# Expert blocks of 64 rows, two experts to a step in the column halves of TensorE

## The reference, cut to what matters

```python
x = x + _L1_ffn_ref(_layernorm(x), ...)      # x is 8 x 100 rows of 512

def _L1_ffn_ref(x, gate_w, gate_b, bias, w1, b1, w2, b2):
    E, TOP_K, D, H = (8, 2, 512, 352)
    xf = x.reshape(-1, d)                                      # 800 rows
    scores = xf @ gate_w.T + gate_b + bias
    top_scores, top_idx = jax.lax.top_k(scores, TOP_K)         # two experts for each row
    gates = jax.nn.softmax(top_scores, axis=-1)
    comb = jnp.sum(jax.nn.one_hot(top_idx, E) * gates[..., None], axis=1)
    h = jax.nn.silu(jnp.einsum('td,ehd->teh', xf, w1) + b1)
    y = jnp.einsum('teh,edh->ted', h, w2) + b2
    return jnp.einsum('ted,te->td', y, comb)
```

## Time and profile before

| what | value |
|---|---|
| median of 3 runs | 660.88 us (657.59 to 663.14) |
| the profiled execution's own time | 661.93 us |
| its span, first to last instruction | 660.0 us |
| PE busy | 553.8 us, 84% of the span |
| DVE busy | 360.5 us, 55% |
| ACT busy | 267.8 us, 41% |
| POOL busy | 194.6 us, 29% |
| mean granted TensorE clock | 0.913 of full speed |

### The profile page before, as it was taken

One profiled execution on the slowest core, in us unless ns is written; L12 is line 12 of the kernel. 1 busy time (PEld: TensorE's weight loads), 2 busy tenths in 40 slices (PEclk: granted clock), 3 DMA queues, 4 the chain that ended last, 5 costly groups with the idle time before them and its releaser, 6 DMA issues.

```text
span 660.0 us, 10081 instructions
## 1 busy us (share of the span) xinstructions
PE 553.8 (84%) x3342; PEld 341.3 (52%) x3342; DVE 360.5 (55%) x989; ACT 267.8 (41%) x611; POOL 194.6 (29%) x237
## 2 busy tenths in 40 slices
PE   4889695999999999869998998998840699999980
PEld 2454343545555555436766776676630455555540
DVE  4453777667676685267778677777353222222210
ACT  1027771412222232158988677775310122222220
POOL 1010303123123321143446455542705021221220
PEclk9969986999999999979999899896755799999996
DMA  8994770322231200130533123312513245445425
GB/s 324 298 419 119 253 235 0 128 94 70 93 129 51 93 1 0 61 111 13 189 99 111 54 58 111 100 57 83 159 45 103 66 82 96 77 86 97 75 39 131
DMA packets 32663, 72.74 MB, mean 110 GB/s; under 512 B 4042, under 2 KB 19434, under 8 KB 30562
## 3 DMA queue, kind: packets, MB, share of 16 engines
q1 hardware_dynamic: 28198, 63.48, 29.6%
q0 software_dynamic: 4416, 8.63, 8.1%
HBM read 46.40 MB, written 27.33 MB: 112 GB/s over the span
## 4 chain that ended last, share of the span: by engine, by line
PE 59%; DVE 19%; DMA 7%; issue 5%; POOL 4%; ACT 4%; SPq 1%; POOLq 0%; DVEq 0%; ACTq 0%
PE ps L818 9%; PE ps L1123 8%; PE ps L1109 8%; PE ps L812 7%; PE ps L893 4%; DMA w1s<-in_win 4%; PE ps L952 4%; PE ps L876 4%; PE ps L1055 3%; DVE sN L1449 2%; PE ps L944 2%; PE ps L965 2%; ACT hTe L781 1%; POOL g L497 1%; DVE VS L1190 1%
## 5 line engine op out<-in xcount | busy, mean ns | idle before, releaser
L812 PE MATMUL ps<-CT,wkS 128*128 128x364 f32 x224 | 77.8, 501 | 9.3 <-DMA wkS<-in_wk 9.3
L728 ACT ACTIVATE pE<-sN,nmx 100x361 f32<-100x361 f32 x128 | 77.7, 607 | 6.2 <-DVE nmx L1449 6.1
L818 PE MATMUL ps<-wvS,CT 128*121 128x512 f32 x168 | 77.0, 607 | 0.0
L1449 DVE CUSTOM_DVE_ANT_0 sN<-ps,maskS 100x361 f32<-100x361 f32 x128 | 62.0, 531 | 11.3 <-PE ps L944 5.8
L952 PE MATMUL ps<-ident,pE 100*121 100x100 f32 x384 | 63.2, 294 | 1.3 <-ACT pT L719 1.1
L606 POOL DMA_INDIRECT sums_out<-yb,backI x20 | 31.1, 1554 | 109.7 <-ACT yb L791 105.7
L952 PEld LDWEIGHTS ps<-ident,pE 100*121 100x121 f32 x384 | 51.9, 200 | 21.5 <-issue 20.2
L812 PEld LDWEIGHTS ps<-CT,wkS 128*128 128x128 f32 x224 | 44.7, 204 | 35.6 <-issue 14.8
L1123 PE MATMUL ps<-VS,hTe 118*128 x120 | 56.7, 609 | 5.5 <-ACT hTe L781 5.5
L719 ACT COPY pT<-ps 121x300 f32<-121x300 f32 x128 | 51.8, 404 | 22.5 <-PE ps L952 22.3
L1574 DVE TENSOR_TENSOR hb<-ps,b1B 128x352 f32<-128x352 f32 x20 | 10.5, 524 | 88.2 <-PE ps L1109 88.2
(11 more groups left out here) (248 smaller groups left out, 958.5 us busy)
## 6 DMA issues: line engine op xcount, KB each, us to landing
slots_in<-zeros SPq DMA_DIRECT2D x8, 1848.0 KB, 8.9
VS<-in_w SPq DMA_DIRECT2D x6, 1024.0 KB, 30.1
CT<-in_ew SPq DMA_DIRECT2D x8, 704.0 KB
VS<-in_ew SPq DMA_DIRECT2D x8, 672.0 KB
xin<-slots_in SPq DMA_DIRECT2D x20, 264.0 KB, 2.8
CT<-in_ctxT SPq DMA_DIRECT2D x7, 728.0 KB, 11.9
ahead<-in_w SPq DMA_DIRECT2D x2, 1024.0 KB, 34.0
summB<-summary_rows SPq DMA_DIRECT2D x8, 200.0 KB
```

The source lines that it names most:

```text
L728: act.activation(pE[0:S, q, 0:T], sN[0:S, q, 0:T], ACT.Exp, scale=-1.0, bias=nmx[0:S, h_:h_ + 1], accum_out=sums[0:S, j, h_:h_ + 1]).then_ ...
L812: mm = pe.matmul(ps[:, at, 0:TP], wkS[:, k, m * P:(m + 1) * P], ctx(b)[:, k * TP:(k + 1) * TP], start=(k == 0), stop=(k == KC - 1))
L818: mm = pe.matmul(ps[0:TC, at, :], ctx(b)[:, k * TP + c * TC:k * TP + (c + 1) * TC], wvS[:, k, :], start=(k == 0), stop=(k == KC - 1))
L1449: dve.tensor_tensor_reduce(out=sN[0:S, q, 0:T], in0=ps[0:S, q, 0:T], in1=maskS[0:S, j, 0:T], scale=-1.0, scalar=3.4e38, op0=ALU.add, op1=A ...
```

## The change

A block is now 64 rows (`BR`), and there are `(1600 + 8 * 63) // 64 = 32` of them. A step handles two blocks, in general of different experts: the first in rows 0 to 63, the second in rows 64 to 127 of the same tiles. So there are `STEPS = 16` steps in place of 20. Each half has its own matrix products, with 64 stationary columns and its own weights; the first half's weights are addressed through a register as before, the second half's are first copied by VectorE to `w1B` and `w2B`. Since a step can now hold the same row twice (once for its first expert and once for its second), the second choice is added to rows of their own (`SECOND` onward in `sums_out`, zeroed early), and both parts are read to SBUF, added and stored at the end, in two column pieces (70% and 30%). The regions of `slots_in` are laid out anew: 13 blocks of 64 rows for each expert in place of 7 of 128.

```diff
+BR = P // 2
+NBLK = (B * S * TOPK + E * (BR - 1)) // BR
+STEPS = NBLK // 2
-RB = B * S // P + 1
+RB = -(-B * S // BR)
+SECOND = B * S + P
+LIN = B * S * D // P
+LIN_CUT = LIN * 7 // 10
...
+            sp.dma_start(sums_out[SECOND:SECOND + B * S].rearrange("(p r) (q c) -> p (r q) c", r=10, q=2),
+                         zeros[0:B * S // 10, 0:D // 2].unsqueeze(1).to_broadcast([B * S // 10, 20, D // 2]))\
+              .then_inc(sem("slots_zero"), 16)
...
-            for s in range(NBLK):
+            for s in range(STEPS):
                 if s > 1:
                     sp.wait_ge(sem("x_taken"), s - 1)
-                load_block(s)
+                load_block(s, 0)
+                load_block(s, 1)
...
-            sp.dma_start(out.rearrange("b s d -> (b s) d"), sums_out[0:B * S]).then_inc(sem("x_kept"), 16)
-            sp.wait_ge(sem("x_kept"), 16 * (B + 1))
+            for i, at in enumerate(lin_parts):
+                sp.dma_start(x_lin[:, at], linear(sums_out[0:B * S])[:, at]).then_inc(sem(f"x_in{i}"), 16)
+                sp.dma_start(s_lin[:, at], linear(sums_out[SECOND:SECOND + B * S])[:, at]).then_inc(sem(f"x_in{i}"), 16)
+            for i, at in enumerate(lin_parts):
+                sp.wait_ge(sem("x_taken"), STEPS + i + 1)
+                sp.dma_start(linear(out.rearrange("b s d -> (b s) d"))[:, at], x_lin[:, at]).then_inc(sem("x_kept"), 16)
+            sp.wait_ge(sem("x_kept"), 16 * (B + 2))
...
                     for k in range(KC):
-                        mm = pe.matmul(ps[:, 2 + j, 0:EH], xT[:, j, k, :], CT[:, e, k * EH:(k + 1) * EH],
-                                       start=(k == 0), stop=(k == KC - 1))
+                        for w, rows in zip((CT[:, e, k * EH:(k + 1) * EH], w1B[:, j, k * EH:(k + 1) * EH]), halves):
+                            mm = pe.matmul(ps[rows, 2 + j, 0:EH], xT[:, j, k, rows], w,
+                                           start=(k == 0), stop=(k == KC - 1))
...
                     for c in range(3):
-                        mm = pe.matmul(ps[:, 7 - j, :], hTe[0:EC, 1 - j, c, :], vs(e)[0:EC, c * D:(c + 1) * D],
-                                       start=(c == 0), stop=(c == 2))
+                        for w, rows in zip((vs(e)[0:EC, c * D:(c + 1) * D], w2B[0:EC, 1 - j, c * D:(c + 1) * D]), halves):
+                            mm = pe.matmul(ps[rows, 7 - j, :], hTe[0:EC, 1 - j, c, rows], w,
+                                           start=(c == 0), stop=(c == 2))
...
+                ch(dve.scalar_tensor_tensor(out=z[0:S, lo:hi, C_TOK:ZW], in0=hot[0:S, 1, lo:hi], scalar=float(SECOND),
+                                            in1=z[0:S, lo:hi, C_TOK:ZW], op0=ALU.mult, op1=ALU.add))
...
             def copy_x(s, j):
                 dve.wait_ge(sem("x_turned"), s + 1)
-                dve.tensor_copy(xT[:, j].rearrange("p k s -> p (k s)"), ps[:, j, :]).then_inc(sem("xT"), 1)
+                dve.tensor_copy(xT[:, j].rearrange("p k s -> p (k s)"), ps[:, j, :])
+                e = block_expert(mybir.EngineType.DVE, s, 1)
+                if s > 1:
+                    dve.wait_ge(sem("h_mm"), s - 1)
+                dve.tensor_copy(w1B[:, j], CT[:, e, 0:KC * EH]).then_inc(sem("xT"), 1)
...
                 if within(s, 0):
-                    e = block_expert(mybir.EngineType.DVE, s)
-                    take_x(s, j, e)
+                    es = [block_expert(mybir.EngineType.DVE, s, half) for half in range(2)]
+                    for half, rows in enumerate(halves):
+                        take_x(s, j, es[half], rows, half)
+                    if s > 1:
+                        dve.wait_ge(sem("y_mm"), s - 1)
+                    dve.tensor_copy(w2B[0:EC, j], vs(es[1])[0:EC, 0:3 * D])
                     alone(dve, ("h_mm", s + 1))
-                    dve.tensor_tensor(hb[:, j], ps[:, 2 + j, 0:EH], b1B[:, e, :], ALU.add).then_inc(sem("h_biased"), 1)
+                    for half, rows in enumerate(halves):
+                        ins = dve.tensor_tensor(hb[rows, j], ps[rows, 2 + j, 0:EH], b1B[rows, es[half], :], ALU.add)
+                    ins.then_inc(sem("h_biased"), 1)
...
+            for i, at in enumerate(lin_parts):
+                dve.wait_ge(sem(f"x_in{i}"), 32 * (STEPS // 2) + 32)
+                dve.tensor_tensor(x_lin[:, at], x_lin[:, at], s_lin[:, at], ALU.add).then_inc(sem("x_taken"), 1)
```

More of the change, by code:

```diff
@@ L161, in block_kernel @@
         need, own = sb(rr, "need", [P, 6, E]), sb(rr, "own", [1, E])
-        blk_e, blk_p, blk_q, blk_no = (sb(rr, n_, [1, NBLK, E]) for n_ in ("blk_e", "blk_p", "blk_q", "blk_no"))
         blk_f = sb(rr, "blk_f", [1, 4, NBLK])
@@ L197, in block_kernel @@
         xin, xT = sb(cc, "xin", [P, 2, ZW]), sb(cc, "xT", [P, 2, KC, P])
-        vacant = sb(cc, "vacant", [P, NBLK])
-        share, backI = sb(cc, "share", [P, NBLK]), sb(cc, "backI", [P, NBLK], I32)
+        vacant = sb(cc, "vacant", [P, STEPS])
+        share, backI = sb(cc, "share", [P, STEPS]), sb(cc, "backI", [P, STEPS], I32)
         hb, hs, hTe = sb(cc, "hb", [P, 2, EH]), sb(cc, "hs", [P, 2, EHP]), sb(cc, "hTe", [P, 2, 3, P])
         yb = sb(cc, "yb", [P, 2, D])
+        w1B, w2B = sb(cc, "w1B", [P, 2, KC * EH]), sb(cc, "w2B", [P, 2, 3 * D])
+        blk_e, blk_p, blk_q, blk_no = (sb(cc, n_, [1, NBLK, E]) for n_ in ("blk_e", "blk_p", "blk_q", "blk_no"))
         cc.close()
@@ L250, in blocks @@
         def blocks(body):
-            for s in range(NBLK + 1):
+            for s in range(STEPS + 1):
                 body(s, s % 2, s // 2)
@@ L258, in within, with block_expert @@
         def within(s, ahead):
-            return s + ahead < NBLK
-        def block_expert(engine, s):
-            return nc.values_load(blk_x[0:1, bass.ds(s, 1)], engines=[engine], min_val=0, max_val=E - 1,
+            return s + ahead < STEPS
+        halves = (slice(0, BR), slice(BR, P))
+        x_lin = XR[:].rearrange("p b d -> p (b d)")
+        s_lin = z[:].rearrange("p b w -> p (b w)")
+        lin_parts = (slice(0, LIN_CUT), slice(LIN_CUT, LIN))
+        def block_expert(engine, s, half):
+            return nc.values_load(blk_x[0:1, bass.ds(2 * s + half, 1)], engines=[engine], min_val=0, max_val=E - 1,
                                   skip_runtime_bounds_check_because="it is a count held to E - 1 when made")
@@ L393, in _, with load_block, linear @@
             keep_x(B - 1)
[L395 to L396 removed]
+            def load_block(s, half):
+                n = nc.values_load(blk_r[0:1, bass.ds(2 * s + half, 1)], engines=[mybir.EngineType.SP], min_val=0, max_val=E * RB,
                                    skip_runtime_bounds_check_because="it is a sum held to E * RB when made")
[L398 removed]
+                sp.dma_start(xin[halves[half], s % 2], slots_in.rearrange("(n p) w -> n p w", p=BR)[n]).then_inc(sem(f"x_in{s % 2}"), 16)
             sp.wait_ge(sem("block_table"), 1)
             sp.wait_ge(sem("sent"), 16 * TOPK * B)
[L402 removed]
+            for s in range(STEPS):
                 if s > 1:
                     sp.wait_ge(sem("x_taken"), s - 1)
[L405 removed]
+                load_block(s, 0)
+                load_block(s, 1)
+            def linear(rows):
+                return rows.rearrange("r d -> (r d)").rearrange("(p c) -> p c", p=P)
             for j in range(2):
[L408 to L410 removed]
+                sp.wait_ge(sem(f"y_out{j}"), 16 * (STEPS // 2))
+            for i, at in enumerate(lin_parts):
[5 more added lines that the diff above has]
+            sp.wait_ge(sem("x_kept"), 16 * (B + 2))
         @block.gpsimd
@@ L600, in _ @@
             g.wait_ge(sem("x_kept"), 16 * B)
-            for t in range(NBLK):
+            for t in range(STEPS):
                 g.wait_ge(sem("y_copied"), t + 1)
@@ L1532, in _ @@
             dve.wait_ge(sem("counts"), 1)
-            ch(dve.tensor_scalar(need[:, 0], ps[:, 4, 0:E], 1.0 / P, 0.5 - 0.5 / P, ALU.mult, ALU.add))
+            ch(dve.tensor_scalar(need[:, 0], ps[:, 4, 0:E], 1.0 / BR, 0.5 - 0.5 / BR, ALU.mult, ALU.add))
             ch(dve.tensor_scalar(need[:, 1], need[:, 0], MAGIC, None, ALU.add))
@@ L1559, in copy_x @@
                 dve.wait_ge(sem("x_turned"), s + 1)
-                dve.tensor_copy(xT[:, j].rearrange("p k s -> p (k s)"), ps[:, j, :]).then_inc(sem("xT"), 1)
-            def take_x(s, j, e):
-                dve.tensor_copy(share[:, s:s + 1], xin[:, j, bass.ds(D + e, 1)])
-                ch(dve.tensor_scalar(vacant[:, s:s + 1], xin[:, j, C_TOK:C_TOK + 1], 0.0, part[:], ALU.is_equal, ALU.mult))
-                dve.tensor_scalar(backI[:, s:s + 1], xin[:, j, C_TOK:C_TOK + 1], vacant[:, s:s + 1], -1.0, ALU.add, ALU.add)\
-                   .then_inc(sem("x_taken"), 1)
+                dve.tensor_copy(xT[:, j].rearrange("p k s -> p (k s)"), ps[:, j, :])
@@ new lines, in copy_x, with take_x @@
+                e = block_expert(mybir.EngineType.DVE, s, 1)
+                if s > 1:
+                    dve.wait_ge(sem("h_mm"), s - 1)
```

(9 more changed lines are left out.)

41 lines of the change are left out of this document (19 added, 22 removed).

## The result

The changed kernel took 652.16 us (median of 4 runs, 648.73 to 654.12) against 661.01 for the kernel before (4 runs, 657.59 to 663.14). The ratio is 0.9861 [0.9826, 0.9897], so 1.0 to 1.7% faster. The profiled execution took 654.12 us, with a span of 652.3, which is 7.7 less than the 660.0 of before. It was the slowest of its four, so 7.7 is less than the 8.9 between the medians.

What follows compares the result with a forecast made beforehand. The loop was taken as bound by TensorE, 6.19 us a step. -111.4 + 14 x 6.4 + 2.6 + 0.3 + 10.0 = -8.9 us took the profiled 661.93 to 653.0, median 652.0; range 645 to 668.

Steps and rivals of the forecast that it cites:

- The sum: Whole kernel: loop, start and end terms together give -8.9 us, for a median of 652.0 us.
- 1 and 2, fewer steps and P: Loop: 18 periods of 6.19 us become 14 of P, the step time, 6.4 us with paired halves priced as one.
- 3, VectorE: Loop: added copies, bias and `take_x`, 3.1 us more against 4.5 of waiting, cost nothing; slack before the product 0.5 us.
- the slow price of `w2B`: VectorE in a step: this copy at the two-tensor operation's rate, about 1.8 us in place of 0.98.
- 4, the scatter: GpSimd: waiting for the previous scatter's landing costs nothing, since two are 5.54 us apart at the end, below the step time.
- 5, ahead of the loop: Before the loop: added operation, second load, weight copies, second bias and clock cost 2.6 us in all, between 1.5 and 4.
- 6, behind the loop: After the loop: bias and width change 0.3 us; reading, adding and storing both parts 17.2 for 7.5, taken as 10 more.
- the lag of passes: Loop products: second half's first record waits for the first half's second; step 7.1 us, +9.8, 662 us; chance 0.12.
- the partial overlap: L1109 and L1123: halves overlap only in part; at x = 0.26 the step is 7.7 us, total 670; chance 0.12.
- VectorE was not late: Loop: rival that slow or blocked copies make `xT` last; step 6.7 to 7.0 us, 656 to 660 us; chance 0.10.
- The end was cheaper and not dearer: After the loop: rival that the end costs 14 to 16 us in place of 10, 656 to 658; chance 0.08.
- slower by 1%: Loop: outcome given to halves overlapping only in part, 1% lost at a step of 7.5 us; chance 0.12.

Runs made afterwards that it cites:

- free scatters: Changed kernel without a scatter's wait for the landing of the one before, with separate spare rows for empty places of odd steps; 651.81 us, ratio 0.9838.
- the kernel with two copies: Changed kernel with another copy of w1B's size, to a tile nobody reads, made ahead of w1B in each step; 657.07 us in one run.
- the kernel with early copies: Changed kernel with w1B and w2B copied ahead of the bias's wait, and for the first two blocks ahead of the loop; 649.89 us, ratio 0.9839.
- the kernel with the second array alone: Kernel before, still 20 steps of 128 rows, with only second choices added to their own array and the changed kernel's end; 671.54 us, ratio 1.0161.
- the one with four pieces: Changed kernel with the final add cut into four column pieces (40, 30, 20 and 10%) in place of two; 650.52 us in one run.
- a half in a row: Changed kernel with all products of a step's first half issued before those of the second, in place of alternating; 673.29 us in one run.
- the warm clock: Changed kernel with idle TensorE products, eleven before the first turning of x and two behind the second block's; 650.14 us, ratio 0.9827.
- two by two: Changed kernel with products ordered two of the first half, then two of the second, in place of one and one; 655.09 us in one run.
- the combined kernels: Changed kernel with early weight copies after the sends, 12 and 2 idle products, and non-waiting scatters; 644.65 us with two end pieces, 643.22 with four.

## Why the prediction was right

**The sum** gave -8.9 and the span shows -7.7; 652.0 was forecast and 652.16 measured. The loop, the largest term, was right by its mechanism and its size. Two terms around it were off, by +2.4 ahead of it and -1.2 behind, and half cancelled. That the median came within 0.2 us is luck: the executions of either kernel lie 5.4 us apart and more.

**1 and 2, fewer steps and P.** The term of the loop was right within 0.1 us, but not by its parts. The pair at the price of one was right, and the rows on mixing were good evidence for it, though with quarters. P was 6.29 and not 6.4. The change of width that is exposed cost 0.16 us, which the gap of 0.14 us behind the mixing had foretold well; the covered one cost nothing, as reckoned, and the second product became 0.05 shorter, which I hadn't reckoned. The 1.5 us saved so were used up by the second block's product at half the clock: from it to the second product of block 0 are 5.36 us, in a steady step 3.49 (554.71 to 558.20 in the chain), so 1.9 lost, of which 0.2 are lost at the full clock too (3.72 us with free scatters). I had put the clock into the start's term and not after it.

**3, VectorE.** `w1B` took 894 ns for a predicted 920 and `w2B` 961 for 980, the bias 0.52 each. The slack, 0.5 in the prediction, is 0.63 to 0.7 by the kernel with two copies. The copies cost nothing in the loop, which the kernel with early copies shows as well. Two figures of that part were added up carelessly: the work that VectorE gets more is 3.0 us by its own terms and not 3.1, and the slow price of `w2B` would be 1.7 and not 1.8. Nothing hangs on either.

**4, the scatter.** No cost in the loop, as predicted. At the end the wait for the landing before does cost 1.7 us. The kernel before waits for a landing there too, so it isn't part of the change.

**5, ahead of the loop.** Mis-sized: +5.0 for +2.6, beyond the 4 that I had as the upper bound. Of it 1.5 are there at the cast of `slotI` (498.15 for 496.63). The added operation can make 0.22 of these. The other 1.3 are no cost of the change that any run shows: the kernel with the second array alone, which has the same operation and the same zeros, has the cast at 497.11, and the one with four pieces, which has all of the change, at 496.27. The first product is 1.9 later against the load's issue, for the second load and `w1B` (0.9 and 0.9 predicted), and the second one 1.6 more, for `w1B` and the second bias (1.4 predicted). Those three terms were right. They and the operation add up to 3.4, and I took 2.6: the 0.8 between was given no reason but that less or more of the first product may be at 1.2 GHz. In the profiled execution that product took 4.98 us, as long as before, and the second one lost the full clock too; with free scatters it took 4.05 us, and the second one kept it. So the sign of this item hangs on the execution, and so does whether the term is 2.4 us off: with free scatters the second block's first product starts at 525.88, +3.2 against before.

**6, behind the loop.** 8.8 for 10.0. The first pieces landed at 8.1 where 7.6 was reckoned, but from the first store's issue to the end were 5.7 us for a reckoned 6.8: what was too dear is the store or the 0.8 us to close, which no row tells apart.

**The rivals.** None came in. Starts 0.01 us apart exclude the lag of passes and the partial overlap in this order; the kernels with other orders show that a lag appears once products of one half stand in a row, so it was a rival of the order and not of the array. VectorE was not late, and the scatter met no copy. The end was cheaper and not dearer. That it might have been slower by 1% had the chance of 0.12; with a half in a row, the change would have been: 673.29 beside 660.43.

## What to carry to other kernels

Two products with 64 stationary columns each run as one if they stand alternately in the program; look at the starts in the trace, a few hundredths apart, before counting on it. When a kernel makes blocks smaller to save padding, reckon what it gives back around the loop with the same care as the step: here 14 of 22 us went there, and 8.9 us by the medians could be had again by moving the copies, the clock, the waits and the cuts. A copy that TensorE waits for can cost twice, if the clock falls meanwhile (1.6 us here, in some executions). Before a gain at such a place is put down to an edit, look how the same place came out in traces that don't have the edit.

## What was not expected of the hardware

- TensorE started a record for a free half of the array ahead of records for the busy half that stand before it in the program: of three, in the first and in the second product and in both other orders.
- A change from 64 back to 128 stationary columns cost 0.16 us where nothing covered it; the change ahead of the second product, where TensorE waits for `hTe`, showed no cost.
- TensorE at 2.4 GHz that stood still was in some executions soon at 1.2 GHz again, and in others not, after waits of the same length. The clock fell after 1.9 us with the warm clock (at 1.2 GHz from 519.4 to 522.8), 2.1 in the changed kernel (528.7 to 532.1) and 2.5 with a half in a row; it stayed over 2.5 us both with free scatters and two by two. In the combined kernels the wait was 1.6 us, and the clock stayed.
- Indirect DMAs that GpSimd issued beside VectorE's float32 copies took 1.33 to 1.75 us for 1.02, and a scatter 1.70 for 1.55.

Left open: whether the second half's weights could be read through a register as the first half's are, which would do without the copies, was not tried; in the loop they cost nothing, ahead of it up to 1.8 us. How far ahead TensorE looks for a free half was seen at two kinds of product only. And what decides whether the clock falls in the wait for `w1B` stays open, with how much of the start's gain belongs to the early copies and how much to the idle products.
